# The second norm of a cross-attention and expert layer, written as a two-source VectorE operation

## The reference

```python
x = x + xattn(layernorm(x), ctx, ctx, Wq, Wk, Wv, Wfc, bfc)
h = layernorm(x)                              # (x - mean) / sqrt(var + 1e-5), along the row of 512
scores = softmax(h @ gate_weight.T)           # 8 experts, group-limited top 2
routed = sum over the chosen experts of w * (silu(h @ gate_w.T) * (h @ up_w.T)) @ down_w.T
shared = (silu(h @ sh_gate_w.T) * (h @ sh_up_w.T)) @ sh_down_w.T
out = x + routed + shared
```

## Time and profile before

| | |
|---|---|
| median of 3 runs | 787.19 us (786.99 to 791.07) |
| span of the profiled execution | 787.2 us; no other time is given for it, so its span stands for its time |
| PE busy | 758.9 us (96%) |
| DVE busy | 581.4 us (74%) |
| ACT busy | 429.7 us (55%) |
| POOL busy | 270.0 us (34%) |

### The profile page before, as it was taken

One profiled execution on the slowest core, in us unless ns is written; L12 is line 12 of the kernel. 1 busy time (PEld: TensorE's weight loads), 2 busy tenths in 40 slices (PEclk: granted clock), 3 DMA queues, 4 the chain that ended last, 5 costly groups with the idle time before them and its releaser, 6 DMA issues.

```text
span 787.2 us, 15937 instructions
## 1 busy us (share of the span) xinstructions
PE 758.9 (96%) x5151; PEld 407.1 (52%) x5152; DVE 581.4 (74%) x1194; ACT 429.7 (55%) x843; POOL 270.0 (34%) x224
## 2 busy tenths in 40 slices
PE   6998989999999989999999999999999999999997
PEld 4553533433433335665655566555555555555553
DVE  5677789999999976999789886555555555546766
ACT  3666579999999973556533553434343343323231
POOL 3353008999994201565300101111111111014431
PEclk9999999999999999999999999999999999999999
DMA  8998856545545798997578565777777777469985
GB/s 312 367 391 238 254 155 205 190 155 200 194 123 171 246 332 313 320 383 258 163 232 226 139 170 145 181 174 175 180 177 181 176 185 174 125 179 276 287 244 151
DMA packets 161784, 172.09 MB, mean 219 GB/s; under 512 B 103680, under 2 KB 117504, under 8 KB 161216
## 3 DMA queue, kind: packets, MB, share of 16 engines
q1 hardware_dynamic: 150012, 128.89, 55.9%
q0 software_dynamic: 11120, 41.43, 16.8%
q10 hardware_dynamic: 596, 1.07, 0.4%
HBM read 105.40 MB, written 42.73 MB: 188 GB/s over the span
## 4 chain that ended last, share of the span: by engine, by line
PE 75%; DVE 14%; DMA 5%; issue 3%; ACT 2%; SPq 1%; DVEq 0%; ACTq 0%
PE psum L1464 30%; PE psum L1476 16%; PE psum L1313 8%; PE psum L1299 6%; PE psum L1227 4%; PE psum L1203 3%; PE psum L1330 2%; DMA sb_weights<-in_wdn 2%; DMA sb_hT<-sb_h 2%; PE psum L1400 2%; PE psum L1179 1%; DVE sb_rows L1899 1%; DVE sb_stats L1891 1%; DVE sb_rows L1889 1%; DVE sb_weights L1925 1%
## 5 line engine op out<-in xcount | busy, mean ns | idle before, releaser
L1464 PE MATMUL psum<-sb_weights,sb_rows 128*128 (+1 forms) x1608 | 250.8, 313 | 0.0
L1464 PEld LDWEIGHTS psum<-sb_weights,sb_rows 128*128 128x128 f16 x1608 | 157.3, 98 | 91.0 <-DMA sb_rows<-xnT_dram 0.2
L1023 ACT ACTIVATE sb_weights<-psum,sb_rows 128x512 f32<-128x512 f32 x256 | 158.4, 685 | 15.1 <-PE psum L1299 13.4
L1696 DVE TENSOR_REDUCE sb_rows<-psum 128x4 f32<-128x1024 f32 x128 | 149.8, 1214 | 5.5 <-PE psum L1227 5.5
L1476 PE MATMUL psum<-sb_weights,sb_hT 128*128 (+1 forms) x630 | 147.4, 379 | 2.7 <-DMA sb_hT<-sb_h 2.0
L892 POOL DMA_INDIRECT sb_rows<-xn_rows,sb_slot_tok x39 | 38.5, 986 | 217.6 <-DVE sb_rows L2285 147.7
L1476 PEld LDWEIGHTS psum<-sb_weights,sb_hT 128*128 128x128 f16 x630 | 61.3, 98 | 68.3 <-DMA sb_hT<-sb_h 2.8
L1092 ACT ACTIVATE psum<-psum 128x352 f32<-128x352 f32 x71 | 31.8, 448 | 113.0 <-DVE psum L1946 104.8
L1299 PE MATMUL psum<-sb_weights 50*128 50x512 f16 x256 | 89.0, 385 | 3.0 <-ACT sb_weights L1023 2.6
L1313 PE MATMUL psum<-sb_weights 128*32 128x256 f32 x1024 | 81.6, 390 | 0.0
L1227 PE MATMUL psum<-sb_weights 48*128 48x256 f16 x512 | 71.8, 272 | 0.6 <-DVE sb_rows L1696 0.6
(11 more groups left out here) (266 smaller groups left out, 1018.0 us busy)
## 6 DMA issues: line engine op xcount, KB each, us to landing
sb_weights<-in_wgu SPq DMA_DIRECT2D x20, 704.0 KB, 7.2
sb_weights<-in_wgu POOLq DMA_DIRECT2D x20, 704.0 KB, 5.6
sb_weights<-in_wdn SPq DMA_DIRECT2D x17, 768.0 KB, 5.9
slot_y<-sb_rows SPq DMA_DIRECT2D x39, 256.0 KB, 2.3
sb_weights<-q_parts SPq DMA_DIRECT2D x96, 64.0 KB, 2.4
x_dram<-sb_rows SPq DMA_DIRECT2D x24, 256.0 KB, 4.6
q_parts<-sb_weights SPq DMA_DIRECT2D x16, 256.0 KB, 4.3
sb_rows<-in_x POOLq DMA_DIRECT2D x16, 256.0 KB, 4.5
```

Of the source, the lines that this page charges most:

```text
L1023: nc.scalar.activation(probs[G % 2][:, kt, pair * 512:(pair + 1) * 512], bank[4 + f % 2], ACT.Exp, scale=exp_scale[:, n:n + 1]).then_inc(e ...
L1464: mm = nc.tensor.matmul(bank[GU_BANKS[par][which]][:, 0:F], x_T[:, xp * D + k * P:xp * D + (k + 1) * P], gu(wp, k, which), start=(k == 0 a ...
L1696: nc.vector.tensor_reduce(to[:, :, j // UB, :, j % UB, qt], psum[:, banks[qt] * 512:(banks[qt] + 2) * 512] .rearrange("p (a h k) -> p a h ...
```

## The change

The norm was a `tensor_scalar` with two scalars per partition: subtract the mean, multiply by the reciprocal deviation. It becomes a `scalar_tensor_tensor`: the mean stays a scalar per partition, and the reciprocal deviation is the second source, a view of the one column repeated 512 times along the row (no copy of it is made). Destination, waits and semaphore are the same.

```diff
--- before.py
+++ after.py
@@ -1896,8 +1896,8 @@
                 dve.wait_ge(std_done, t + (BLOCKS + 1))
                 newton(link, 1, rstd[:, 0:1])
                 dve.wait_ge(xn2_stored[s], n * 16 + FREE)
-                nc.vector.tensor_scalar(xn2_sb[s], x2_sb[s], mv[:, 0, 0:1], rstd[:, 0:1],
-                                        ALU.subtract, ALU.mult).then_inc(ln2_done, 1)
+                nc.vector.scalar_tensor_tensor(xn2_sb[s], x2_sb[s], mv[:, 0, 0:1], rstd[:, 0:1].broadcast_to([P, D]),
+                                               ALU.subtract, ALU.mult).then_inc(ln2_done, 1)
 
             def down_scales(link):
 
```

## The result

The changed kernel is slower, by 0.4 to 0.7% in three sets of runs, each beside the kernel before:

| set | changed | before | ratio, 95% interval |
|---|---|---|---|
| first | 795.98 us (6 runs) | 789.32 us (6 runs) | 1.0069 [1.0044, 1.0093] |
| second | 791.09 us (12 runs) | 788.23 us (35 runs) | 1.0051 [1.0029, 1.0074] |
| third | 795.00 us (12 runs) | 790.13 us (17 runs) | 1.0043 [1.0018, 1.0069] |

The account below looks back on a forecast made before the run. The prediction took DVE's norm line, held by POOL in seven tiles, to set PE's pace in the token stage; 0.41 us each gave 2.9, taken as 2.8, so 787.2 + 2.8 = 790.0 us, range 783.8 to 791.2.

Parts of the forecast that it names:

- What bounds the stage: Token stage, tiles 5 to 14: DVE's norm line sets PE's pace, though PE's own work is only 6% behind.
- The new form is held like the old: Seven tiles' norms: the two-input form still waits to the end of POOL's operation; chance 0.60, 788.6 to 791.1 us.
- The argument from likeness: Norm beside POOL: taken as held because nearest to the old form, L1899, in what it touches in SBUF.
- The tail (a), 0.205 us: Each of seven held norms: the extra 0.205 us comes after POOL's release, the front part being hidden under the wait.
- the high bound: Held norms: the streaming left after release, 0.28 us, doubles; (a) and (b) about 0.28 each, 3.9 us in all.
- POOL's side (b), 0.205 us for each of seven tiles: The tile before's longer norm delays POOL's L801 or L858, so L811 or L862 and the held norm end 0.205 later.
- So the shift passes on one to one: From tile 5 to the kernel's end, PE is later by the whole sum: 787.2 + 2.8 = 790.0 us.
- Base and range: Whole kernel: base 787.19 us, the median of the runs; range 783.8 to 791.2 us.
- the first (not held): Norm passes beside POOL and PE becomes the bound: at most 3.6 us gained, 3.0 taken, 784.2 us; chance 0.25.
- The flip: Norms of tiles 4, 6, 8, 10 fall behind L801 and wait 2.5 us for its end; about 792 us; chance 0.04.
- Half rate: Two 4-byte SBUF streams run at half rate, 0.53 us more per norm; 10 us more, 797; chance 0.03.
- Partly held: Norm's wait on POOL only partly kept, or POOL delayed and DVE not; gain and loss cancel, 786 to 788; chance 0.08.

Follow-up runs that it names:

- PSUM: Against the changed kernel: the reciprocal deviation is written to a PSUM column and repeated from there, one wide input in SBUF; 785.36 us, ratio 0.9961 to the kernel before.
- write only: POOL's scaling and subtracting in the token stage replaced by zero fills, in the changed kernel (787.01 us) and in the kernel before (783.44 us).

## Why the prediction was wrong, point by point

- **What bounds the stage:** right. In the changed kernel PE starts the transposes 0.05 to 0.06 us after the norm in the held tiles, and when the hold is gone (PSUM, write only) PE's pace of 5.15 us a tile shows at once.
- **The new form is held like the old:** right, in the same seven tiles, and the second SBUF stream is what is held (PSUM: no hold). The argument from likeness was weaker than it read: the old form is held by fills that only write, the new one is not, so the two are not held by the same thing. The row at L2321 gave the free price to the nanosecond, 752.
- **The tail (a), 0.205 us:** mis-sized. It is 0.27 (1.89 us for seven), close to the 0.28 of the high bound: what is left after POOL's release doubles, from 0.28 us to 0.54. The part hidden under the wait is not the same in both forms: 0.547 - 0.28 = 0.27 us of the old one, 0.752 - 0.54 = 0.21 of the new. That adds 1.89 - 1.43 = 0.46 us.
- **POOL's side (b), 0.205 us for each of seven tiles:** right in size where it acts (L801 +0.20 us) and counted too often. In the kernel with the new form in the free tiles only, the transposes come later by 0.42 us at tile 5 (the share of tiles 2 and 4), by 0.20 to 0.22 at each of tiles 6, 8, 10 and 12, and 0.08 of that is lost again at tiles 13 and 14. Tile 14's share was counted twice, since L858 waits for tile 13's norm, whose tail is already in the sum. 1.16 us in place of 1.43. The two errors partly cancel, 3.05 against 2.8.
- **"So the shift passes on one to one":** this is the step that failed. The shift of the waits passed on, but the step took PE's waits as time alone and put at nothing what they could do to the granted clock. In three of four profiles of the changed kernel the clock was at its lower level right behind them, for 1.67 us more; in none of three of the kernel before. The rows of before gave a granted clock of 1.00 at this place with waits of 0.43 and 0.29 us; the prediction should have asked what more waiting there does to it. Whether the waits are the cause stays open, and so do about 2 us of the first set's 6.7.
- **Base and range:** the base was a median of three runs, 787.19, and larger sets gave 788.2 to 790.1. The upper end of 791.2 left room for neither that nor the clock: with the base of the first set, the forecast's own +2.8 already gives 792.1. This part of the miss is scatter of the base and says nothing on the mechanism.
- **Rivals:** the first (not held) did not happen in this kernel, and its working was right: with one input in PSUM it gives -3.4 us in the stage (forecast at most -3.6, taken -3.0) and 0.9961. The flip did not occur; the lead is still 0.29 us (348.55 against 348.84). Half rate did not occur. Partly held did not occur.
- **Chances:** slower by over 0.5% had 0.13, for the flip and the half rate. It came by neither.
- **A reading:** tile 13's norm ends 0.32 us into L858 (371.53 + 2.95 = 374.48, against 374.16), not 0.27; the sum does not use it.

## What to carry to other kernels

Where a VectorE operation takes one of two times and the long ones end a fixed bit after a GpSimd operation, suspect that it is held. Here a rewrite helped only where it took away the access that is held: a second operand from PSUM did (785.4 us), a second operand in SBUF did not, even as one column repeated. Price a held operation by what is left after the release, and let the longer one delay the other engine too. Where the engine that bounds the kernel waits longer, even by tenths of a microsecond, look at its granted clock in the stretch behind the wait, and do not count on the clock staying as it was.

## What the runs showed that I had not expected

- The old form (one input, SBUF to SBUF) is held by POOL's fills, which read nothing; the new form, with two SBUF inputs, is not (1.50 against 0.75 us for tile 9).
- Freed of its own hold, the norm hands it to the next operation with two SBUF inputs: L1925 goes from 1.67 to 2.62 us.
- The granted clock falls at the end of the stage in four of five profiles where PE's wait at tile 14 is 0.55 us or more, and in none of eight where it is 0.29 or less.
